# A table spreads the preparation of an image over 48 other slots: the 17 last units of one image's convolution and all units of the next

## What is computed

```python
x = x + _L0_conv_ref(_gn(x), ...)   # channel attention: 192 x 192 Gram matrix, softmax, w_v, w_out
x = x + _L1_conv_ref(_gn(x), ...)   # deformable 3x3 convolution, batch norm over all images, gelu
```

```python
offset = jnp.clip(_conv(x, off_w, off_b), -max_off, max_off)
mask = 2.0 * jax.nn.sigmoid(_conv(x, mask_w, mask_b))
y = _deform_conv(x, offset, mask, proj_w, proj_b)
```

## Time and profile before

| | us |
|---|---|
| median of 3 runs | 4050.97 (4041.22 to 4051.61) |
| profiled execution | 4042.66, its span 4041.0 |
| PE busy | 3563.3 (88% of the span) |
| DVE, ACT, POOL busy | 2633.4, 2109.1, 1412.3 |
| image 0 prepared alone | until about 122 |
| last pass | from about 3820 |

### The profile page before, as it was taken

The page is one execution under the profiler, slowest core; times in us unless marked ns, Lnnn a source line. Parts: engine busy times, 40 slices in busy tenths (PEclk is TensorE's granted clock), DMA queues, the critical chain, the costliest instruction groups (busy, mean ns, idle before and its releaser), DMA issues.

```text
span 4041.0 us, 108743 instructions
## 1 busy us (share of the span) xinstructions
PE 3563.3 (88%) x38307; PEld 3052.9 (76%) x38307; DVE 2633.4 (65%) x5773; ACT 2109.1 (52%) x4790; POOL 1412.3 (35%) x1165
## 2 busy tenths in 40 slices
PE   3999999999999999999999999999999999999700
PEld 2788887888888788888878888887887878788700
DVE  3566776676667667676766766676666667766622
ACT  1555554555555455555545555555555555555432
POOL 1333333343433333333333333333333333333311
PEclk8999999999999999999999999999999999999955
DMA  2000000000000000000000000000001000000299
GB/s 63 20 10 28 29 28 20 28 28 18 20 28 28 20 28 28 28 10 28 28 21 28 28 28 10 29 28 28 20 28 28 28 11 28 28 20 18 69 374 322
DMA packets 50763, 170.48 MB, mean 42 GB/s; under 512 B 9665, under 2 KB 10881, under 8 KB 50177
## 3 DMA queue, kind: packets, MB, share of 16 engines
q1 hardware_dynamic: 39584, 136.75, 11.1%
q0 software_dynamic: 7168, 25.17, 1.6%
q10 hardware_dynamic: 3424, 0.90, 0.1%
HBM read 87.29 MB, written 75.50 MB: 40 GB/s over the span
## 4 chain that ended last, share of the span: by engine, by line
PE 62%; DVE 14%; issue 11%; ACT 5%; DMA 4%; DVEq 2%; ACTq 1%; SPq 1%; POOL 0%; POOLq 0%
PE sps L680 9%; PE acc L697 6%; PE acc L699 6%; PE acc L698 6%; PE l L609 4%; DVE zl L1141 3%; PE zps L666 3%; PE zps L670 3%; PE zps L667 3%; PE zps L668 3%; PE zps L669 3%; DVE sl L1147 2%; DMA xn<-x_scratch 2%; ACT sh L890 2%; DVE ych L1201 2%
## 5 line engine op out<-in xcount | busy, mean ns | idle before, releaser
L1324 POOL TENSOR_TENSOR sT<-ay,bx 128x768 f32<-128x768 f32 x768 | 1149.1, 1506 | 1400.8 <-PE sps L680 1333.5
L1147 DVE TENSOR_TENSOR sl<-sps,sh 128x384 f16<-128x384 f32 x1536 | 846.8, 551 | 597.9 <-ACT sh L890 595.0
L697 PE MATMUL acc<-zh,sh 128*128 128x192 f16 x4608 | 1139.7, 247 | 0.3 <-ACT ypm L911 0.3
L698 PE MATMUL acc<-zl,sh 128*128 128x192 f16 x4608 | 1139.7, 247 | 0.0
L699 PE MATMUL acc<-zh,sl 128*128 128x192 f16 x4608 | 1139.7, 247 | 0.0
L890 ACT CAST sh<-sps 128x384 f16<-128x384 f32 x1536 | 740.5, 482 | 728.4 <-PE sps L680 723.5
L866 ACT CAST zh<-zps 128x288 f16<-128x288 f32 x1536 | 619.7, 403 | 652.5 <-PE zps L670 625.5
L680 PE MATMUL sps<-eye,sT 128*128 128x128 f32 x4608 | 790.9, 281 | 155.7 <-DVE sl L1147 96.1
L1141 DVE TENSOR_TENSOR zl<-zps,zh 128x288 f16<-128x288 f32 x1536 | 693.4, 451 | 356.9 <-ACT zh L866 351.8
L680 PEld LDWEIGHTS sps<-eye,sT 128*128 128x128 f32 x4608 | 536.1, 142 | 308.5 <-DVE sl L1147 168.9
L698 PEld LDWEIGHTS acc<-zl,sh 128*128 128x128 f16 x4608 | 453.6, 98 | 18.5
(11 more groups left out here) (201 smaller groups left out, 6466.3 us busy)
## 6 DMA issues: line engine op xcount, KB each, us to landing
xin<-in_x SPq DMA_DIRECT2D x32, 512.0 KB, 5.3
xin<-in_x SPq DMA_DIRECT2D x64, 256.0 KB, 5.9
x_scratch<-x SPq DMA_DIRECT2D x32, 512.0 KB, 2.8
y_scratch<-ych SPq DMA_DIRECT2D x32, 512.0 KB, 2.7
zh<-y_scratch SPq DMA_DIRECT2D x20, 512.0 KB, 10.9
zl<-x_scratch SPq DMA_DIRECT2D x20, 512.0 KB, 12.4
out<-zh POOLq DMA_DIRECT2D x20, 512.0 KB, 8.8
x_scratch<-x SPq DMA_DIRECT2D x32, 256.0 KB, 3.5
```

The costliest lines, as they stand in the source:

```text
L697: pe.matmul(acc[:, 0:C], s_h, zh[:, j, ky, z], start=start and kx == 0, stop=False)
L698: pe.matmul(acc[:, 0:C], s_h, zl[:, j, ky, z], start=False, stop=False)
L1147: dve.tensor_tensor(one(sl), sps[u % 2][:, 0:3 * P], one(sh), ALU.subtract).then_inc(s_lo, 1)
L1324: pool.tensor_tensor(sT[:, p % ST_RING].rearrange("p k (r x) -> p k r x", r=R), a, x_, ALU.mult)\
```

## The change

The calls of part0 in the units go through `beside`, with a table `PLAN` from unit to stages. Negative keys are units of the image before: -17 is unit 31. So while image b is convolved, units 0 to 30 carry stages 19 to 46 of image b + 1, and units 31 to 47 stages 0 to 18 of image b + 2. `left` counts how many images still follow (2, 1 or 0).

```diff
+        PLAN = {-17: (0,), -16: (1,), -15: (2,), -14: (3, 4), -13: (5,),
...
+                7: (25,), 8: (26,), 9: (27,), 10: (28,), 11: (29,), 12: (30,), 13: (31,), 14: (32,), 15: (33,),
+                16: (34,), 17: (35,), 19: (36,), 21: (37,), 22: (38,), 23: (39,), 24: (40,), 25: (41,), 26: (42,),
...
+        LEAD = -min(PLAN)
+        FIRST_UNITS = UNITS - 10
+        def squeezed(units, span, offset):
+            out = {}
+            for at in range(span):
+                out.setdefault(offset + at * units // span, []).extend(PLAN.get(at - LEAD, ()))
+            return out
+        FIRST_PLAN = squeezed(FIRST_UNITS, LEAD + max(PLAN) + 1, 0)
+        FIRST_LEAD = squeezed(UNITS - FIRST_UNITS, LEAD, FIRST_UNITS)
+        def beside(part0, u, b, par, left):
+            if left >= 1:
+                for stage in FIRST_PLAN.get(u, ()) if first(b) else PLAN.get(u, ()) if u >= 0 else ():
+                    part0(stage, b + 1, 1 - par)
+            if left >= 2:
+                for stage in FIRST_LEAD.get(u, ()) if first(b) else PLAN.get(u - UNITS, ()):
+                    part0(stage, b + 2, par)
...
-            part1(0, 0, True)
-            with eng.Fori(1, NB - 2, 2) as b:
-                part1(b, 1, True)
-                part1(b + 1, 0, True)
-            part1(NB - 1, (NB - 1) % 2, False)
+            part1(0, 0, 2)
+            with eng.Fori(1, NB - 4, 2) as b:
+                part1(b, 1, 2)
+                part1(b + 1, 0, 2)
+            part1(NB - 3, 1, 2)
+            part1(NB - 2, 0, 1)
+            part1(NB - 1, 1, 0)
...
-                    if u % 12 == 4 and u < 36:
-                        column_hats(u // 12 + 1, b, par)
+                    if u in (4, 14, 22):
+                        column_hats((4, 14, 22).index(u) + 1, b, par)
...
-                if u == 33:
-                    if not first(b):
-                        dve.wait_ge(off_ps, b)
-                    move(0, b, par)
...
                 if u == 35:
                     dve.wait_ge(xn_lo, 4 * b + 4)
+                    if not first(b):
+                        dve.wait_ge(off_ps, b)
+                    move(0, b, par)
+                if u == 36:
                     move(1, b, par)
-                if u == 36:
+                if u == 37:
                     move(2, b, par).then_inc(x2_moved, 1)
...
-                    if u == 7 and i is None:
+                    if u == (17 if left else 7) and i is None:
                         offset_distance(b, par)
...
-                    if 5 <= u < 7 and i is None and not first(b):
-                        y_stats(u - 3, b - 1, 1 - par)
-                    if u in (38, 39) and i is None:
-                        y_stats(u - 38, b, par)
+                    if u in (2, 3) and i is None and not first(b):
+                        y_stats(u, b - 1, 1 - par)
+                    if u in (35, 37) and i is None:
+                        y_stats((u - 35) // 2, b, par)
...
-                        for u in (2 * p - 4, 2 * p - 3):
-                            part0(u, b + 1, 1 - par)
+                    for u in (2 * p - 4, 2 * p - 3):
+                        beside(part0, u, b, par, left)
+                for u in range(UNITS - 4, UNITS):
+                    beside(part0, u, b, par, left)
```

More of the change, by code:

```diff
@@ L354, in image_alone @@
                 part0(u, b, 0)
-            part1(b, 0, False, i)
+            part1(b, 0, 0, i)
             far_pass(b, i)
@@ L741, in far_pass, with part1 @@
                     mm.then_inc(fyt_ps, 1)
-            def part1(b, par, more, i=None):
+            def part1(b, par, left, i=None):
                 if first(b) or i is not None:
@@ L751, in part1 @@
                         turn_s(u + 2, b)
-                    elif more:
+                    elif left:
                         turn_s(u + 2 - UNITS, b + 1)
                     convolve(u, b, par)
-                    if u == 9 and not more and i is None:
+                    if u == 9 and not left and i is None:
                         offset_max(b)
@@ L762, in part1 @@
                         turn_y(u // 12 - 1, b)
-                    if more:
-                        part0(u, b + 1, 1 - par)
+                    beside(part0, u, b, par, left)
                 turn_y(3, b)
```

11 lines of the change are left out of this document (5 added, 6 removed), and 3 rows, old and new, of the table PLAN.

## The result

| | before | changed |
|---|---|---|
| median of the runs | 4050.97 us (3 runs, 4041.22 to 4051.61) | 4288.45 us (4 runs, 4284.59 to 4296.45) |
| ratio, 95% interval | 1 | 1.0597 (1.0569 to 1.0625) |
| profiled execution, its span | 4042.66, 4041.0 | 4296.45, 4294.8 |

A fourth run of the kernel before, 4744.94 us, was slow and is left out. The change makes the kernel 237 us slower. I had said 4085, 34 us slower, with a range up to 4140: the sign was right, the size far off.

A forecast was written before the change was run, and what follows sets the result against it. PE's work plus PE's waits bound the kernel; the terms sum to +1.1 us per image, +34 over 30 images, with -5 and +12 once: 4084 from the profiled 4042.7, said as 4085 us, range 3990 to 4140.

The forecast's parts named there:

- stage 4: Unit 34, one unit after stage 2: PE waits for `mv`, +2.5 us per image, bounds 1.5 and 2.9.
- At no cost: POOL's steps cost nothing: column distance at unit 25 is covered by three `sT` made ahead, `load_x` by its early issue.
- Rival 3: PE's clock falls behind its new wait at unit 34, one unit 1.66 us longer per image: 4135 us, chance 0.12.
- Once only: -5: The loop makes 14 turns instead of 15, so 13 PE stops instead of 14, saving 5 us once.
- The first image, +12: First image squeezes 48 slots into 38 units and 17 into 10; PE waits +12 us once, between 0 and 25.
- Hats, -0.5: Hats at units 24 to 30 instead of 40 to 46: -0.5 us per image, bounds -0.7 and +1.5.
- The moves, +0.4: Units 14 to 21: DVE's moves meet `sT`, waits of 3.7 become 4.1 us per image, bounds 2.4 and 4.6.
- rival 1: DVE's moves fall beside `sT`, each taking 0.85 us: faster, about 3982 us, chance 0.2.
- stages 21, 47 and the residues: Stage 21 two units after stage 20 -0.8, end of unit 47 -0.3, residues at 38 and 40 -0.2 us per image.

The follow-up runs named there:

- turn_shift: The changed kernel with 16 semaphore increments that nobody waits for ahead of the loop on PE: 4219.31 us, ratio 1.0424 to the kernel before.
- respaced: The changed kernel with a new table: stages 0 to 2 in units 24 to 26, pairs spaced, moves at 19, 21, 23: 3934.13 us, ratio 0.9727.
- moves_alone: The changed kernel with `offset_distance` in unit 13 and `scale_y` in units 20, 32, 44, not directly ahead of a move: 4226.13 us, ratio 1.0443.

## Why the prediction was wrong

The way of reading held: the kernel's time is PE's work plus what single stages make PE wait, and nearly all of the loss was found unit by unit. That the sign came out right owes most to stage 4, whose wait was forecast by its mechanism and its size. These steps failed:

- **"At no cost" and the list of moved stages.** I compared the distances between stages 2 and 4 and between 20 and 21 and did not do so for 10 and 12. It costs 1.5 us per image, 45 us. The residue takes 2.0 us here and a unit 1.68; the earlier trace rows had a residue of 1.72 and the earlier trace rows the unit, so even the rows at hand left it too little room.
- **Rival 3's chance of 0.12.** The forecast put the clock at nothing. It does fall behind a lone wait of 1.9 us, and the loss is larger than rival 3's 1.66: 2.4 per image, 72 us. The evidence was a gap between 1.08 and 3.3 us, and a wait inside the gap deserved an even chance, not one in eight. The Trainium skill ("TensorE: Matmul & The Clock Gate", What's actually happening) has idle time of PE bring the throttled state; the trace agrees with it here, by the 0.50 behind unit 34.
- **"Once only: -5" for the loop.** I counted turns and took the price of one from the earlier trace rows as fixed. With a second stop and the low clock behind it a turn costs 7.3 us and not 5.2: 13 x 7.3 against 14 x 5.2 is +22, not -5. turn_shift shows that all but 2.7 of the 7.3 belong to where the loop begins. No sum of stages gives this, so the price of a turn should have had a range.
- **The first image, +12, between 0 and 25.** 27 of waits: just beyond the upper end.
- **Hats, -0.5.** It was +0.6, near the middle of my bounds (-0.7 to +1.5), and for the reason given for the upper one. POOL, after its wait for `off`, makes three `sT` in a row, and `ay` times mask waits for one of them; ahead of it stand POOL, then DVE, then PE:

```profile
2334.32 4.57 POOL L1352 TENSOR_TENSOR sT<-ay,bx 128x768 f32<-128x768 f32 x3
...
2337.58 1.62 DVE L1148 TENSOR_TENSOR ay<-ay,mask 128x288 f32<-128x288 f32 x1
...
2339.73 0.55 PE L711 MATMUL sps<-eye,sT 128*128 128x128 f32 x3 [1.15 <-DVE sl L1176]
```

- **The moves, +0.4.** `sT` does hold one copy in each of two moves, as forecast against rival 1, but the size was low: +1.0 with the offset convolution's wait, which the 3.7 us of the forecast included, and their 4.7 us stand just above its upper bound of 4.6.

These steps held: stage 4 (+2.2, and 0.2 in unit 33, for +2.5, within 1.5 and 2.9); stages 21, 47 and the residues, each to 0.1 us. The misses together are 45 + 72 + 27 (turns) + 15 (first image) + 33 (hats, 1.1 x 30) + 18 (moves, 0.6 x 30) = 210 us, where 203 lie between 4085 and 4288; the last three images pay only a part of what is taken 30 times here. Rival 1 described another table than this one: in respaced all copies of L1037 take about 0.18 us, and the kernel gains 112 us.

## What to carry to other kernels

When work is spread by a table, list every producer and consumer pair on different engines with its distance in slots, before and after, and not only those that the change seems to be about: where the distance is shorter than the producer's time, the bounding engine waits in every image. Give jobs that share a port a fixed place against the other engine's long instruction, and look again after each move of a neighbour. A part of the price of a loop's turn belongs to the program's layout, so a change that moves instructions across the loop's start needs its stops counted anew. Here 16 idle instructions ahead of the loop took 69 us off, most of it in the turns.

## What the runs showed of the hardware

- A wait of 1.9 us on PE can cost as much again in clock. Of two waits of 1.90 and 1.91 us one is followed by 1.00 and the other by 0.50. In the change all of the images 1 to 28 are hit; in turn_shift 9 of them are spared, every second one from image 3 to image 19. What decides it stays open.
- A turn of the loop has one or two stops of PE, most of them 1.4 to 3.7 us long, without any releaser. In the changed kernel 16 or 48 idle instructions ahead of the loop took the second away, with nothing changed in the loop.
- A DVE copy of 96 elements per partition takes 0.17 us or 1.4, one of 992 elements 0.42 or 1.46, depending on the `sT` beside it. With the hold gone from one move, and `scale_y` gone from ahead of it, its unit took 1.68 us instead of 3.07 (moves_alone).
